# A selective-scan block with a quantised FFN: VectorE's two C products of a unit become one instruction, and one more unit's product goes to VectorE

## The reference, cut to what matters

```python
delta = softplus(dlt @ W_dt.T + b_dt)
deltaA = exp(delta[..., None] * A)
deltaBx = delta[..., None] * Bm[:, :, None, :] * xc[..., None]
def step(h, inp):
    dA, dBx, c = inp
    h = dA * h + dBx
    return (h, einsum('bdn,bn->bd', h, c))
_, ys = lax.scan(step, h0, (deltaA, deltaBx, Cm))
y = ys + xc * D
```

## Time and profile before

| | |
|---|---|
| runs of the kernel (3) | 5140.6, 5141.44, 5143.02 us; median 5141.44 |
| profiled execution, first to last instruction | 5139.8 us |
| median less this span | 1.6 us |
| VectorE busy | 4789.5 us (93%) |
| TensorE busy | 4759.9 us (93%) |
| GpSimd busy | 3832.3 us (75%) |
| ScalarE busy | 3336.0 us (65%) |
| first and last scan start | 121.0 and 3520.1 us |
| TensorE's mean granted clock | 0.975 of full |

### The profile page before, as it was taken

The page is one execution under the profiler, slowest core; times in us unless marked ns, Lnnn a source line. Parts: engine busy times, 40 slices in busy tenths (PEclk is TensorE's granted clock), DMA queues, the critical chain, the costliest instruction groups (busy, mean ns, idle before and its releaser), DMA issues. The chain is left out here.

```text
span 5139.8 us, 67238 instructions
## 1 busy us (share of the span) xinstructions
PE 4759.9 (93%) x21964; PEld 3283.1 (64%) x21964; DVE 4789.5 (93%) x5476; ACT 3336.0 (65%) x7037; POOL 3832.3 (75%) x1722
## 2 busy tenths in 40 slices
PE   8799899998999989999999898967999999999999
PEld 3555555555555555555555555555888888888888
DVE  8999999999999999999999999997888888888887
ACT  3777877777777787777777877765444444444442
POOL 6999999999999999999999999994322322322231
PEclk9899999999999999999999999988999999999999
DMA  7555565655656556566566666554010011001000
GB/s 268 173 198 194 189 204 185 196 195 191 199 188 200 195 186 204 186 198 196 188 199 188 194 199 191 187 172 156 25 38 31 31 34 35 31 31 37 31 31 29
DMA packets 402675, 745.79 MB, mean 145 GB/s; under 512 B 44083, under 2 KB 44211, under 8 KB 402198
## 3 DMA queue, kind: packets, MB, share of 16 engines
q1 hardware_dynamic: 401590, 738.08, 43.7%
q0 software_dynamic: 736, 3.41, 0.2%
HBM read 698.05 MB, written 43.26 MB: 144 GB/s over the span
## 5 line engine op out<-in xcount | busy, mean ns | idle before, releaser
L717 POOL TENSOR_TENSOR slot<-du,b_row 128x1024 f32<-128x1024 f32 x1024 | 2397.9, 2379 | 0.2
L1050 DVE TENSOR_TENSOR_SCAN decays<-decays,state,slot 128x512 f32<-128x512 f32 x1376 | 1686.6, 1270 | 61.6 <-POOL slot L717 50.3
L917 ACT ACTIVATE decays<-delta,rate 128x512 f32<-128x512 f32 x2048 | 1385.0, 687 | 50.6 <-DVE slot L998 2.2
L1111 PE MATMUL work_ps<-h_t,win 128*128 128x512 f32 x2048 | 981.8, 627 | 137.5 <-ACT delta L853 109.1
L1188 PEld LDWEIGHTS y_ps<-ident,slot 128*128 128x128 f32 x8192 | 946.2, 143 | 238.2 <-issue 177.9
L1188 PE MATMUL y_ps<-ident,slot 128*128 128x128 f32 x8192 | 1020.9, 277 | 42.6 <-POOL slot L724 30.7
L1574 POOL TENSOR_TENSOR hq<-hid,qinv 128x1408 f32<-128x1408 f32 x63 | 163.5, 2596 | 1001.7 <-DVE qinv L1600 1001.7
L1057 DVE TENSOR_TENSOR slot<-decays,c_row 128x512 f32<-128x512 f32 x1376 | 870.8, 673 | 0.0
L724 POOL TENSOR_TENSOR slot<-slot,c_row 128x1024 f32<-128x1024 f32 x336 | 797.7, 2374 | 81.8 <-ACT state L906 79.7
L1050 DVE TENSOR_TENSOR_SCAN slot<-decays,state,slot 128x512 f32<-128x512 f32 x672 | 819.0, 1263 | 4.0 <-POOL slot L717 2.2
L1111 PEld LDWEIGHTS work_ps<-h_t,win 128*128 128x128 f32 x2048 | 393.7, 201 | 590.0 <-issue 493.1
(11 more groups left out here) (274 smaller groups left out, 7356.9 us busy)
## 6 DMA issues: line engine op xcount, KB each, us to landing
b_row<-b_c_rows SPq DMA_DIRECT2D x1024, 256.0 KB, 3.9
c_row<-b_c_rows SPq DMA_DIRECT2D x1024, 256.0 KB, 3.8
win<-in_w_in SPq DMA_DIRECT2D x256, 256.0 KB, 4.4
xt<-in_x SPq DMA_DIRECT2D x16, 1024.0 KB, 7.1
xr<-in_x SPq DMA_DIRECT2D x64, 256.0 KB, 4.4
x_after_mamba<-xr SPq DMA_DIRECT2D x64, 256.0 KB, 4.6
xa<-x_after_mamba SPq DMA_DIRECT2D x64, 256.0 KB, 3.0
xres<-x_after_mamba SPq DMA_DIRECT2D x64, 256.0 KB, 2.7
```

The source lines that it names most:

```text
L717: pool.tensor_tensor(slot[:, u % SLOTS, :, :], du[:, p % 2, :, :], two(b_row[:, u % BC_RING, :]), ALU.mult).then_inc(S["ub_ready"], 1)
L917: act.activation(decay[u % 2][:, i, :], delta[:, p % 2, i, :], ACT.Exp, scale=rate[:, 2 * p + i, n:n + 1]).then_inc(S["decay_ready"], 1)
L1050: dve.tensor_tensor_scan(d if u in DVE_C else h, d, h, state[:, 2 * p + i, n:n + 1], ALU.mult, ALU.add).then_inc(S["scan_done"], 1)
L1111: op = pe.matmul(dst[:, :], win[:, i % WIN_RING, k, :], h_t[:, k, :], start=(k == 0), stop=(k == KT - 1))
```

## The change

`DVE_C` gets unit 1 as its 44th entry, so that unit's C product is VectorE's and no longer GpSimd's. VectorE's product is one instruction of 128x1024 over both blocks, with the C row broadcast over them, and waits for both scans. ScalarE saves both blocks' last columns with one copy in every unit, behind the whole C product where VectorE does it, and both decays follow. `half_used` goes, and `state_saved` counts one a unit.

```diff
@@ -91,7 +91,7 @@
     61: [("load_win", 12, 1)], 63: [("load_win", 13, 1)],
 }
 DVE_C = (
-    2, 3, 4, 6, 8, 9, 11, 12, 14, 15, 16, 19, 20, 21, 22, 24, 26, 27, 29, 30, 31, 34, 35, 36, 38, 39, 41, 42, 43, 44,
+    1, 2, 3, 4, 6, 8, 9, 11, 12, 14, 15, 16, 19, 20, 21, 22, 24, 26, 27, 29, 30, 31, 34, 35, 36, 38, 39, 41, 42, 43, 44,
     45, 47, 48, 51, 52, 53, 55, 57, 58, 59, 60, 61, 63,
 )
 
@@ -480,7 +480,7 @@
                 sem("prep_scales"), sem("prep_scaled"), sem("prep_rounding"), sem("prep_rounded"))
             names = ("x_loaded bc_ready bc_saved cleared ln_ready seed_ready ln_chain xn_ready halo_ready "
                      "xc_ready zs_ready dt_ready "
-                     "u_ready ub_ready decay_ready scan_done half_used state_saved "
+                     "u_ready ub_ready decay_ready scan_done state_saved "
                      "sum_done xd_ready rows_seen part_done part_out").split()
             S = {n: sem(n) for n in names}
 
@@ -517,10 +517,6 @@
                 first = {(k, a): s for k, a, s, _ in ITEMS}
                 order.sort(key=lambda ka: -first[ka])
                 return {BANK[ka]: ka for ka in order}
-
-            def half_used(u, c):
-
-                return c.at(len(DVE_C), sum(v <= u for v in DVE_C))
 
             def c_done(u, c):
 
@@ -719,7 +715,7 @@
 
                     def times_c(u, c):
                         h = slot[:, u % SLOTS, :, :]
-                        wait(pool, S["state_saved"], c.at(2 * UNITS, 2 * u + 2))
+                        wait(pool, S["state_saved"], c.at(UNITS, u + 1))
                         wait(pool, *ring_loaded(c_loaded, c, u))
                         pool.tensor_tensor(h, h, two(c_row[:, u % BC_RING, :]), ALU.mult).then_inc(c_row_used[u % BC_RING], 1)
 
@@ -896,14 +892,11 @@
                             "z_out": z_out, "silu_x": silu_x, "silu_z": silu_z, "x_out": x_out, "softplus": softplus,
                             "y_out": y_out, "xd": skip_out, "residual": residual}
 
-                    def save_state(u, i, c):
+                    def save_state(u, c):
                         p, n = divmod(u, N)
-                        if u in DVE_C:
-                            wait(act, *((S["half_used"], half_used(u, c)) if i == 0 else c_done(u, c)))
-                            act.activation(state[:, 2 * p + i, n:n + 1], decay[u % 2][:, i, T - 1:T], ACT.Copy).then_inc(S["state_saved"], 1)
-                        elif i == 0:
-                            wait(act, S["scan_done"], c.at(2 * UNITS, 2 * u + 2))
-                            act.activation(state[:, 2 * p:2 * p + 2, n], slot[:, u % SLOTS, :, T - 1], ACT.Copy).then_inc(S["state_saved"], 2)
+                        h = decay[u % 2] if u in DVE_C else slot[:, u % SLOTS, :, :]
+                        wait(act, *(c_done(u, c) if u in DVE_C else (S["scan_done"], c.at(2 * UNITS, 2 * u + 2))))
+                        act.activation(state[:, 2 * p:2 * p + 2, n], h[:, :, T - 1], ACT.Copy).then_inc(S["state_saved"], 1)
 
                     def decays(u, i, c):
                         p, n = divmod(u, N)
@@ -912,8 +905,8 @@
                             act.wait_ge(prep_rounded, len(PREP))
                         if n == 0:
                             wait(act, *piece_read("d", 2 * p + i, c))
-                        if exists(cc) and v in DVE_C:
-                            wait(act, S["state_saved"], c.at(2 * UNITS, 2 * (u - 2) + i + 1))
+                        if exists(cc) and v in DVE_C and i == 0:
+                            wait(act, S["state_saved"], c.at(UNITS, u - 1))
                         act.activation(decay[u % 2][:, i, :], delta[:, p % 2, i, :], ACT.Exp,
                                        scale=rate[:, 2 * p + i, n:n + 1]).then_inc(S["decay_ready"], 1)
 
@@ -921,10 +914,10 @@
                         for pos in range(UNITS):
                             v, cc = back(c, pos - 2)
                             saving = exists(cc) and (exists(c) or pos < 2)
-                            for i in range(2):
-                                if saving:
-                                    save_state(v, i, cc)
-                                if exists(c):
+                            if saving:
+                                save_state(v, cc)
+                            if exists(c):
+                                for i in range(2):
                                     decays(pos, i, c)
                             first = c.reg is None and c.off == 0
                             late = [("z_out", j, c) for j in FIRST_Z.get(pos, ())] if first else []
@@ -1042,7 +1035,7 @@
                     def scan(u, i, c):
                         p, n = divmod(u, N)
                         if n == 0 and i == 0:
-                            wait(dve, S["state_saved"], c.at(2 * UNITS, 2 * (N * (p + 1) - UNITS)))
+                            wait(dve, S["state_saved"], c.at(UNITS, N * (p + 1) - UNITS))
                         wait(dve, S["decay_ready"], c.at(2 * UNITS, 2 * u + i + 1))
                         if i == 0:
                             wait(dve, S["ub_ready"], c.at(UNITS, u + 1))
@@ -1050,15 +1043,11 @@
                         dve.tensor_tensor_scan(d if u in DVE_C else h, d, h, state[:, 2 * p + i, n:n + 1],
                                                ALU.mult, ALU.add).then_inc(S["scan_done"], 1)
 
-                    def times_c(u, i, c):
-                        if i == 0:
-                            wait(dve, *ring_loaded(c_loaded, c, u))
-                        wait(dve, S["scan_done"], c.at(2 * UNITS, 2 * u + i + 1))
-                        op = dve.tensor_tensor(slot[:, u % SLOTS, i, :], decay[u % 2][:, i, :], c_row[:, u % BC_RING, :], ALU.mult)
-                        if i == 0:
-                            op.then_inc(S["half_used"], 1)
-                        else:
-                            op.then_inc(c_row_used[u % BC_RING], 1)
+                    def times_c(u, c):
+                        wait(dve, *ring_loaded(c_loaded, c, u))
+                        wait(dve, S["scan_done"], c.at(2 * UNITS, 2 * u + 2))
+                        dve.tensor_tensor(slot[:, u % SLOTS, :, :], decay[u % 2], two(c_row[:, u % BC_RING, :]),
+                                          ALU.mult).then_inc(c_row_used[u % BC_RING], 1)
 
                     def body(c):
                         for pos in range(UNITS):
@@ -1070,8 +1059,7 @@
                                 if cc.reg is None and cc.off == 0:
                                     prep_between(step, arg)
                             if exists(c) and pos in DVE_C:
-                                times_c(pos, 0, c)
-                                times_c(pos, 1, c)
+                                times_c(pos, c)
                             for step, arg, cc in steps(DVE_STEPS, c, (pos, 1)):
                                 HAVE[step](arg, cc)
                                 if cc.reg is None and cc.off == 0:
```

## The result

The changed kernel takes 5226.02 us (5225.43 to 5227.79), the kernel before 5141.02 beside it: a ratio of 1.0165 [1.0151, 1.0179]. That is 85 us more, where 32 were forecast and 59 was the end of the range. The sign was right and the size was not.

The account below looks back on a forecast made before the run. VectorE was taken to set the pace of the scan stretch, at times waiting for GpSimd. Per chunk +3.4 - 3.0 + 1.4 gave +1.8 to +2.0 us, times 16 = +31 us: 5173 us, range 5147 to 5200.

Parts of the forecast that it names:

- (1): Scan stretch, VectorE: two C products become one in 43 units a chunk; +2.2 us per chunk, bounds -2.4 to +3.0.
- (2): Unit 1's C product moves from GpSimd to VectorE: +1.24 us per chunk on VectorE, GpSimd loses 2.3 us.
- (3): VectorE's waits for GpSimd at units 3, 4, 8, 14 go, 0.3 us left at 21: -3.0 us per chunk.
- (4): ScalarE's decays come later, new VectorE waits at units 4, 22, 54: +1.4 us per chunk, bounds 0.7 to 2.6.
- the own wait: VectorE's merged product waits for its own engine's scan directly ahead of it: 0.11 us each.
- GpSimd's lead: GpSimd, without unit 1's product, is 2.3 us earlier from unit 4 on, removing VectorE's waits: 3.0 us per chunk gained.
- the three units named: Units 4, 22 and 54: new VectorE waits for ScalarE of 0.6, 0.3 and 0.5 us per chunk.
- Rival A: VectorE's wait on its own last instruction is free: -1.8 us per chunk, 5113 us; chance 0.09.
- B: ScalarE's new waits don't arise and all waits for GpSimd go: +0.1 us per chunk, 5143 us; chance 0.09.
- C: ScalarE becomes the pace, seven places with little slack cost 0.3 us each: +34 us more, 5207 us; chance 0.12.

Follow-up runs that it names:

- lagged: Kernel before plus unit 1 on VectorE; in 14 units a chunk, merged C product placed behind the next unit's first scan: 5136.73 us (nine units: 5130.44).
- the run that changes one number: Kernel before, first of VectorE's two C products waits for both scans, written behind the wait for the C row: 5246.0 us, ratio 1.0204.

## Why the prediction was wrong

Per chunk, forecast against measured:

| step | forecast | measured |
|---|---|---|
| (1) merged product in 40 plain units, three gated ones | +2.2 us | +5.9: 40 x 0.152 - 3 x 0.06 |
| (2) unit 1 | +1.24 | +1.3 |
| (3) waits for GpSimd | -3.0 | -3.2: 52.5 to 1.8 us in all |
| (4) waits for ScalarE | +1.4 | +1.4: decays +0.73, gates +0.64 |
| sum | +1.9 | +5.4; the stretch grew by 5.3 |

**Step (1) failed, in the size of one term:** the own wait was costed at 0.11 us from the earlier trace rows, as 0.03 us of gap for 0.08 of overlap, and it is 0.22, a unit of 3.70 us where the merged product with its wait covered makes 3.49. Of this 0.19 is the gap of 0.10 us for an overlap of 0.09, with 0.07 in it for a wait that the sequencer does by itself; the other 0.02 is the product's record, 1.225 us behind an own wait and 1.205 in the lagged units. The nearest rows were a chain with a single wait; the new instruction has two. I had put this term's bounds at 0 and 0.12 us, so the range couldn't hold the time either. The range was also narrower than its own terms: their upper ends, +0.5, +1.0 and +1.2 us over the forecast, add up to some 5215 us and not to 5196; the 5226 measured lie beyond both. With the two waits in the better order it was 5183.23 us, 10 us from the forecast: a plain unit of 3.63 us for 3.61 is 15 us more in 640 units, and the waits came to some 6 us less than forecast. So the mechanism was right (own wait against overlap, GpSimd's lead as the cover) and one term was too small by half.

**Steps (2) and (3) held, and (4) in its sum.** The waits for GpSimd at 3, 4, 8, 14 are gone; at 21 too, since VectorE comes late enough itself, where I had left 0.3 us. The waits for ScalarE's decays came at the three units named, in the changed kernel in these rows of VectorE's timeline at units 4 and 54:

```profile
1446.36 2.46 DVE L1043 TENSOR_TENSOR_SCAN decays<-decays,state,slot 128x512 f32<-128x512 f32 x2 [0.48 <-ACT decays L910]
...
1616.82 1.28 DVE L1043 TENSOR_TENSOR_SCAN slot<-decays,state,slot 128x512 f32<-128x512 f32 x1 [0.34 <-ACT decays L910]
```

They are shorter than forecast (0.6 and 0.5), as a slower VectorE needs its decays later: with the same copies and the product in two instructions they are 0.79 and 0.43 us. That the sum is 1.4 all the same is partly luck. The gate of unit 4 waits 8.0 us in all for TensorE's projection (L1129), 0.8 before, and no step of the prediction names that wait.

**Rival A** (the own wait is free) is refuted by the run that changes one number: +105 us. The rule of the Trainium skill, "VectorE: DVE Perf Modes", section "The DRAIN you can't avoid", is that the semaphore between VectorE instructions costs nothing extra; here it holds only where the wait is for something already done. The kernels side by side, units 42 and 43, from a unit's first scan to the next unit's, mean over the chunks:

| plain unit on VectorE | wait covered | own wait, written first | own wait, written second |
|---|---|---|---|
| two products | 3.55 us | 3.70 | 3.77 |
| merged | 3.49 (lagged) | 3.63 | 3.70 |

Down each column the merge saves 0.06 or 0.07 us; along each row the own wait costs 0.15 us where it is written first and 0.22 or 0.21 where it is written second. In the changed kernel the two together lose 0.15.

**Rivals B and C** did not come about: decays hold VectorE at three places in each chunk, not at none and not at ten.

## What to carry to other kernels

Before merging two instructions, look at what each waits for: two halves that take turns hide each other's waits, and one whole instruction behind its producer does not. When an instruction has several waits, find out which of them the instruction itself carries, and let that be the one that ends last; here it was the first in the program. A gain on one engine is worth only what the others leave of it: the same moved product gave 11 us in one kernel and cost 11 in the other.

## What was unexpected about the hardware

The place of a wait in the program costs 0.07 us each time on VectorE: gaps of 104 and 34 ns behind the same scan. ScalarE shows nearly the same two figures. Its copy of two states (L906 in the kernel before, which adds 2 to its semaphore) starts 94 ns after the scan it waits for, with a separate wait in the sequencer's records, and the same copy in the changed kernel (L899, which adds 1) after 34 ns. The traces of the other runs agree.
TensorE's eight matmuls behind an idle time of 5.5 us took 6.00 or 6.57 us, at a granted clock that stayed at half for more or less of them.
